# A graph-attention and four-expert kernel: the maxima over partitions moved behind the experts' low parts, and every engine's order redrawn

## The chip, the cores and the metric

The kernel runs on 1 core of a Trainium2 chip. The metric is the device time of one execution in microseconds. A core has four computing engines, each with its own instruction list that it runs strictly in the order written: TensorE (PE, matrix products), VectorE (DVE), ScalarE (ACT) and GpSimd (POOL). SyncE (SP) only issues DMAs here. The engines meet at semaphores.

## The reference

Four batches of 512 rows with 512 features go through a two-layer graph attention over a context of 512 x 128, and then through a feed-forward part in which row 4g+e belongs to expert e:

```
x = x + xattn(ctx, adj=layernorm(x), W0, ..., W1, ...)      # two attention layers, 8 heads of 64
n = layernorm(x)
gate, up = split(n[rows of e] @ gate_up[e])                 # 512 x 1024 for each of 4 experts
x = x + (silu(gate) * up) @ down[e]
```

The adjacency is the layernormed x, and the mask added to the attention's logits is 1e10 times (adj - 1). A row's softmax therefore puts all its weight on the place of the largest x in that row, wherever the gap to the second largest is big enough. The kernel uses that: it computes y = elu(elu(ctx W0 + b0) W1 + b1) for all rows, finds each row's largest entry, and gathers from y twice by index. On the side it proves that this holds for every row (a bound made of the largest absolute values of the inputs, against each row's gap). A flag with the number of rows so proved decides at the end whether a general program must run; with these inputs it does not.

## The kernel before, in words

**Numbers.** A float32 product is made of three fast products of split numbers: each operand is cut into a high part (a cast) and a low part (the rest), and high x high, high x low and low x high are added. So every operand costs one cast (on ACT: `r_high`, `h_high`, `turned_xn`, `inner_high`) and one subtraction (on DVE or POOL: `r_low`, `h_low`, `turned_low`, `inner_low`), and each 128 x 512 result of depth 512 takes twelve matmuls. "A twelve" is such a group below.

**Stages.** (1) Layer 0, `layer0(b, c)`: 16 products of 128 x 512 for h; ACT and DVE make elu of them (`h_exp_of`, `h_below`, `h_value`). (2) Layer 1, `layer1(n)`: 16 twelves; n = 4b+t is a block of 128 rows of batch b. A bank is first filled by ACT with the bias (`seed`), and ACT and DVE make y (`y_exp_of`, `y_value`), which SP stores to a table in memory (`store_y`). (3) DVE finds the largest entry of each row of x (`find_top`, `find_row`, `rows`). POOL issues the indirect DMAs: `follow(b, e)` reads the index of an index, `gather(b, e)` reads rows of the y table and adds them to x of batch b, expert e. (4) For each expert e and batch b: DVE's `x2_stats`, `x2_moments`, POOL's `x2_inverse(e, b)` (the inverse root of the variances; for e > 0 one call serves b and b+1), DVE's `normalize(e, b)`, PE's `turn_xn` (a transpose), ACT's `turned_xn` and DVE's `turned_low`. (5) The experts. Expert 0 is done batch by batch (`first_gate`, `first_up`, `first_inner`, `turn_inner`, `first_down`), so that it can begin when one batch is there; experts 1 to 3 take all four batches in a piece (`gate(e, c)`, `up(e, c)`, `inner(e, c)`, `down_of(e, i)`, `last_down(e, b)`, `output(e, b)`).

**Weights.** 24 blocks of 512 KB, `load_r(r)`, go through a ring of 9 slots. Block r takes the slot of block r-9 and is loaded only when PE has done with that one. Blocks 0 to 5 are of expert 0, 6 to 11 of expert 1, and so on; blocks 9 and 10 are the third and fourth gate-up block of expert 1, 11 is the second half of its down weights, and 12 and 13 are the first two gate-up blocks of expert 2.

**The proof's inputs.** SP loads ctx, W1, W0 and the small vectors again (`again_ctx`, `again_w`); DVE takes maxima along rows (`ctx_maximum`, `small_maxima`), and POOL's `all_maxima` takes them over the 128 partitions with two `partition_all_reduce` calls. x is loaded again too (`again_x(b)`, then `x_stats`). `check_rows` on DVE uses all of it, late in the program.

**What sets the order.** Each engine's list of calls is written out by hand-written statements, one call per line, and so are the `pe.wait_ge` lines between PE's calls and the tables of banks. Tables of numbers say which low parts DVE makes; POOL makes the rest.

Of the kernel before, what the change touches and what calls it, by code (L numbers as in the profile page):

```python
# [20 lines left out]
F32 = mybir.dt.float32  # L21
# [355 lines left out]
def build(nc, x, ctx, W0, a_self0, a_neigh0, b0, W1, a_self1, a_neigh1, b1, gate_up, down, out,  # L377
# [19 lines left out]
    with ExitStack() as stack:  # L397
# [114 lines left out]
        Z_BANK = (2, 4, 7, 2, 7, 3, 0, 4, 6, 2, 6, 1, 6, 2, 5, 0)  # L512
        Y_BANK = (5, 1, 0, 7, 1, 5, 2, 0, 4, 1, 7, 4, 2, 1, 7, 5)
        XN_BANK = (0, 6, 3, 5, 4, 5, 0, 7, 4, 5, 6, 7, 4, 5, 6, 7)
        GATE_BANK = (0, 4, 6, 6, 4, 6, 4, 6, 4, 6, 4, 6, 4, 6, 4, 6)
        UP_BANK = (6, 0, 4, 3, 5, 7, 5, 7, 5, 7, 5, 7, 5, 7, 5, 7)
        IN_BANK = (6, 3, 1, 7)
        DOWN_BANK = (2, 2, 2, 0, 0, 1, 2, 3, 0, 1, 2, 3, 0, 1, 2, 3)
# [120 lines left out]
        def _(sp):  # L639
# [60 lines left out]
            load_r(0)  # L700
            load_b1(0)
            load_w(1)
            load_r(1)
            load_ctx(1)
            load_ctx(2)
            load_r(6)
            load_w(2)
            load_r(4)
            load_x(0)
            load_r(2)  # L710
            load_r(8)
            load_ctx(3)
            load_x(3)
            load_x(1)
            load_x(2)
            load_r(3)
            load_r(5)
            store_y(0)
            store_y(1)
            store_y(2)  # L720
            load_r(7)
            store_y(3)
            store_y(4)
            store_y(5)
            store_f(0)
# [3 lines left out]
            store_f(2)  # L729
            store_y(8)  # L730
            store_y(9)
            store_y(10)
            store_y(11)
            store_y(12)
            store_y(13)
            store_y(14)
            store_f(3)
            store_y(15)
            again_ctx()
            again_w()  # L740
# [5 lines left out]
            load_r(11)  # L746
            again_x(0)
            load_r(15)
            store_out(0, 2)
            load_r(16)  # L750
            again_x(1)
            load_r(14)
            load_r(13)
            store_out(0, 3)
            load_r(18)
            again_x(2)
            load_r(19)
            load_r(17)
            again_x(3)
            load_r(21)  # L760
            load_r(22)
            store_out(1, 0)
            load_r(20)
            store_out(1, 1)
            store_out(1, 2)
            store_out(1, 3)
            load_r(23)
# [12 lines left out]
        def _(pool):  # L780
# [63 lines left out]

            r_low(0)
            r_low(1)
            h_low(1, 0)
# [5 lines left out]
            h_low(2, 1)  # L853
            h_low(2, 2)
            r_low(3)
            r_low(4)
            r_low(6)
            follow(0, 0)
            h_low(2, 3)
            follow(1, 0)  # L860
            follow(1, 1)
            gather(0, 0)
            gather(1, 0)
            h_low(3, 0)
            follow(1, 2)
            follow(2, 0)
            follow(2, 1)
            x2_inverse(0, 0)
            follow(0, 1)
            x2_inverse(0, 1)  # L870
            follow(0, 2)
            gather(2, 0)
            gather(0, 1)
            gather(1, 1)
            gather(2, 1)
            x2_inverse(0, 2)
# [3 lines left out]
            follow(0, 3)  # L880
            gather(3, 0)
            gather(3, 1)
            follow(3, 2)
            follow(3, 3)
            gather(1, 2)
            x2_inverse(0, 3)
            gather(0, 3)
            follow(1, 3)
            x2_inverse(1, 0)
            x2_inverse(1, 2)  # L890
            follow(2, 2)
            gather(1, 3)
            follow(2, 3)
            gather(2, 2)
            gather(3, 2)
            x2_inverse(2, 0)
            gather(2, 3)
            gather(3, 3)
            all_maxima()
            x2_inverse(2, 2)  # L900
            r_low(9)
            inner_low(1, 0)
            r_low(10)
            x2_inverse(3, 0)
            r_low(11)
            r_low(12)
            x2_inverse(3, 2)
            r_low(13)
            r_low(14)
# [288 lines left out]
        def _(dve):  # L1198
# [16 lines left out]
            def h_value(b, c):  # L1215
# [5 lines left out]
                else:  # L1221
                    dve.wait_ge(h_rest, n - KC + 1)
                    if n == KC:
                        dve.wait_ge(b0_made, 1)
# [734 lines left out]
```

## Time and profile before

| | us |
|---|---|
| median of 3 runs | 237.5 (235.0 to 239.65) |
| time of the profiled execution | 237.21 |
| its span, first to last instruction | 235.4 |
| PE busy | 208.7 (89%) |
| DVE / POOL / ACT busy | 152.6 / 112.6 / 98.9 |

The profiled execution is 0.3 us under the median, and its span leaves 1.8 us of its time outside. The page cuts the span into 40 slices of 5.9 us, where a digit is a busy share in tenths. PEclk is the clock granted to TensorE; 9 stands for full speed and 5 for half. The chain lists, in order of time, the work that each thing waited for, back from the end; "issue" is a time for which the profile shows no cause.

### The profile page before, as it was taken

What the parts mean: (1) busy time and instruction counts of PE and PEld (TensorE: products, weight loads), DVE (VectorE), ACT (ScalarE), POOL (GpSimd) and SP (SyncE); (2) the same over time, 40 slices, a digit from 0 to 9 for tenths busy, and PEclk for the clock granted to TensorE, in tenths of its full rate; (3) what the DMA queues carried; (4) which work ended last, traced back from release to release, by engine and by line L of the source; (5) the groups of instructions that cost most, each with busy time, mean ns of one, the idle gap of its engine ahead of it and who ended that gap; (6) DMA issues with size and microseconds to landing.
All of it is one profiled execution on the core that took longest, in us unless ns stands there. A gap on an engine that the chain in (4) does not pass through costs nothing.

```text
span 235.4 us, 2762 instructions
## 1 busy us (share of the span) xinstructions
PE 208.7 (89%) x918; PEld 163.4 (69%) x918; DVE 152.6 (65%) x283; ACT 98.9 (42%) x155; POOL 112.6 (48%) x87
## 2 busy tenths in 40 slices
PE   7989999999998979999800599999999999999990
PEld 3446777768877857888700488888888888888870
DVE  0689999998996369986203997796892633422231
ACT  2899999996533211502350012816216132222100
POOL 2324577989888679585014880621354820020000
PEclk9999999999999999999965599999999999999997
DMA  6999991216449899469940059846263021111005
GB/s 203 354 410 421 410 338 52 90 48 128 140 93 198 192 195 259 95 127 271 325 173 0 0 157 363 265 143 235 89 221 140 0 89 46 45 47 45 0 30 156
DMA packets 15202, 38.78 MB, mean 165 GB/s; under 512 B 2768, under 2 KB 2768, under 8 KB 14160
## 3 DMA queue, kind: packets, MB, share of 16 engines
q1 hardware_dynamic: 12080, 34.10, 40.8%
q0 software_dynamic: 2816, 4.20, 11.7%
q10 hardware_dynamic: 288, 0.26, 0.3%
q8 instruction: 8, 0.13, 0.2%
q14 instruction: 10, 0.08, 0.2%
HBM read 30.16 MB, written 8.40 MB: 164 GB/s over the span
## 4 chain that ended last, share of the span: by engine, by line
PE 44%; DVE 18%; issue 15%; DMA 10%; POOL 8%; ACT 3%; POOLq 0%; SPq 0%
PE bank L1690 25%; PE bank L1704 14%; POOL x_sb L819 4%; DMA y_table<-val 4%; DVE found L1254 3%; DVE top L1250 3%; DVE hexp L1225 3%; DVE val L1244 3%; DMA ff_row<-f_table,f_row 2%; DMA val<-in_ctx 2%; DMA x_sb<-y_table,ff_row 2%; POOL ff_row L807 2%; PE bank L1734 2%; PE bank L1677 1%; PE bank L1640 1%
## 5 line engine op out<-in xcount | busy, mean ns | idle before, releaser
L1690 PE MATMUL bank<-acts,ring 128*128 128x512 f32 x288 | 69.8, 399 | 14.9 <-DVE first_parts L1295 14.9
L1690 PEld LDWEIGHTS bank<-acts,ring 128*128 128x128 f32 x288 | 55.3, 193 | 26.8 <-DVE first_parts L1295 15.1
L794 POOL TENSOR_TENSOR ring<-ring_raw,ring 128x1024 fp32r<-128x1024 f32 x15 | 36.6, 2460 | 27.7 <-ACT ring L930 27.7
L1626 PE MATMUL bank<-wide,acts 128*128 128x512 f32 x192 | 48.9, 408 | 0.6 <-ACT bank L963 0.4
L1626 PEld LDWEIGHTS bank<-wide,acts 128*128 128x128 f32 x192 | 35.7, 188 | 12.3 <-issue 3.1
L1704 PE MATMUL bank<-ring,wide 128*128 128x512 f32 x144 | 34.5, 391 | 0.0
L930 ACT CAST ring<-ring_raw 128x1024 fp32r<-128x1024 f32 x24 | 24.5, 1053 | 16.2 <-DMA ring_raw<-in_down_t 9.3
L1704 PEld LDWEIGHTS bank<-ring,wide 128*128 128x128 f32 x144 | 26.9, 188 | 5.5
L819 POOL DMA_INDIRECT x_sb<-y_table,ff_row x16 | 25.8, 1613 | 8.1 <-issue 3.3
L1026 ACT CAST wide<-hexp 128x512 fp32r<-128x512 f32 x12 | 7.5, 621 | 42.0 <-DVE hexp L1304 42.0
L1651 PE MATMUL bank<-ring,first_xnT 128*128 128x512 f32 x96 | 23.0, 394 | 1.2 <-DVE first_xnT L1284 1.2
L833 POOL TENSOR_TENSOR wide<-hexp,wide 128x512 fp32r<-128x512 f32 x6 | 7.9, 1315 | 31.1 <-ACT wide L1026 31.1
L1276 DVE TENSOR_SCALAR xn<-x_sb,x2mv,rstd 128x512 f32<-128x512 f32 x16 | 11.3, 732 | 16.3 <-POOL rstd L827 15.0
L1651 PEld LDWEIGHTS bank<-ring,first_xnT 128*128 128x128 f32 x96 | 17.7, 188 | 5.0 <-DVE first_xnT L1284 1.4
L807 POOL DMA_INDIRECT ff_row<-f_table,f_row x16 | 18.7, 1171 | 4.2 <-issue 3.6
L1317 DVE SCALAR_TENSOR_TENSOR x_sb<-x_sb,bank 128x512 f32<-128x512 f32 x16 | 10.9, 687 | 12.4 <-PE bank L1704 11.8
L1614 PE MATMUL bank<-ctxT,W_f 128*128 128x512 f32 x32 | 16.8, 624 | 1.3 <-DVE hexp L1219 1.3
L1304 DVE TENSOR_TENSOR hexp<-bank,hexp 128x512 f32<-128x512 f32 x12 | 8.2, 686 | 14.5 <-PE bank L1690 14.5
L1015 ACT ACTIVATE hexp<-bank 128x512 f32<-128x512 f32 x12 | 7.1, 595 | 21.3 <-PE bank L1690 21.3
L1208 DVE TENSOR_TENSOR ring<-ring_raw,ring 128x1024 fp32r<-128x1024 f32 x9 | 13.0, 1462 | 4.4 <-ACT ring L930 4.4
L800 POOL TENSOR_TENSOR acts<-hexp,acts 128x512 fp32r<-128x512 f32 x9 | 12.1, 1370 | 6.5 <-ACT acts L954 6.5
L969 ACT ACTIVATE yexp<-bank,minus_one 128x512 f32<-128x512 f32 x16 | 10.9, 708 | 5.1 <-PE bank L1626 5.1
(87 smaller groups left out, 250.7 us busy)
## 6 DMA issues: line engine op xcount, KB each, us to landing
ring_raw<-in_gate_up_t SPq DMA_DIRECT2D x16, 512.0 KB, 6.4
ring_raw<-in_down_t SPq DMA_DIRECT2D x8, 512.0 KB, 8.0
x_sb<-in_x SPq DMA_DIRECT2D x4, 1024.0 KB, 16.4
y_table<-val SPq DMA_DIRECT2D x16, 256.0 KB, 3.5
out<-x_sb SPq DMA_DIRECT2D x16, 256.0 KB, 2.8
val<-in_x SPq DMA_DIRECT2D x4, 1024.0 KB
ctxT<-in_ctx_t SPq DMA_DIRECT2D x4, 256.0 KB, 8.0
wide_raw<-in_W_t SPq DMA_DIRECT2D x2, 512.0 KB, 8.3
```

Of the source, the lines that this page charges most:

```text
L794: nc.gpsimd.tensor_tensor(ring[:, r % RING, LO, :], ring_raw[:, r % RING, LO, :], ring[:, r % RING, HI, :].bitcast(F32), ALU.subtract).the ...
L800: nc.gpsimd.tensor_tensor(hT[:, b % 2, c, LO, :], hexp[:, n % HEXP, :], hT[:, b % 2, c, HI, :].bitcast(F32), ALU.subtract).then_inc(h_lo_p ...
L807: nc.gpsimd.indirect_dma_start(out=ff_row[:, b, e:e + 1], out_offset=None, in_=f_table[b][:, :], in_offset=bass.IndirectOffsetOnAxis(ap=f_ ...
L819: nc.gpsimd.indirect_dma_start(out=x_sb[:, b, e, :], out_offset=None, in_=y_table[b][:, :], in_offset=bass.IndirectOffsetOnAxis(ap=ff_row[ ...
L930: nc.scalar.copy(ring[:, r % RING, HI, :], ring_raw[:, r % RING, LO, :]).then_inc(r_hi, 1)
L1208: nc.vector.tensor_tensor(ring[:, r % RING, LO, :], ring_raw[:, r % RING, LO, :], ring[:, r % RING, HI, :].bitcast(F32), ALU.subtract).the ...
L1276: nc.vector.tensor_scalar(xn[:, b, :], x_sb[:, b, e, :], x2mv[:, e, b, 0:1], rstd[:, e, b:b + 1], ALU.subtract, ALU.mult).then_inc(xn_made, 1)
L1614: nc.tensor.matmul(bank[Z_BANK[n]][:, :], W0_f[:, c * P:(c + 1) * P], ctxT[:, b, :], start=True, stop=True).then_inc(h_done, 1)
L1626: last = nc.tensor.matmul(bank[Y_BANK[n]][:, :], hT[:, b % 2, c, w, t * P:(t + 1) * P], W1p[:, c, v, :], start=False, stop=(c == KC - 1 an ...
L1651: last = nc.tensor.matmul(bank[(UP_BANK if half else GATE_BANK)[b]][:, :], first_xnT[:, b % 2, k, w, :], ring[:, 0:KC, v, (half * KC + k) ...
L1690: last = nc.tensor.matmul(bank[(UP_BANK if half else GATE_BANK)[KC * e + c]][:, :], ring[:, r % RING, w, col:col + P], xnT[:, (e - 1) % 2, ...
L1704: last = nc.tensor.matmul(bank[DOWN_BANK[B * e + b]][:, :], inner_parts[:, i, w, b * P:(b + 1) * P], ring[:, r % RING, v, (i % 2) * D:(i % ...
```

## The change

Four things are edited; nothing that is computed changes.

1. **POOL's order.** `all_maxima()` stands behind `x2_inverse(2, 2)`, `x2_inverse(3, 0)`, `x2_inverse(3, 2)` and `r_low(9)`, `r_low(10)`, `r_low(12)`, and ahead of `r_low(13)`, `r_low(14)` and the rest. The four `gather(b, 3)` and the `follow` calls move forward.
2. **All other orders.** PE runs `first_gate(0)` between the parts of `layer1(12)`; expert 0's last down products and expert 1's parts are laid out anew. SP loads the ring's blocks in another order, several of them behind `store_y(0)` to `store_y(3)`. ACT runs `first_silu(0)` ahead of `y_exp_of(12)`. The banks are given out anew.
3. **Who makes low parts.** Ring blocks: DVE 9 to 11, POOL 15 to 13. Expert parts of experts 1 to 3: DVE 6 to 8, POOL 6 to 4. h: DVE 7 to 8, POOL 9 to 8.
4. **Batch 0's h.** `h_below` of h(0, 1) and h(0, 3) goes from DVE to ACT, which changes the sign in which these two are kept.

```diff
-        R_LO_DVE = (5, 7, 8, 15, 16, 17, 18, 19, 23)
-        H_LO_DVE = (0, 1, 2, 3, 13, 14, 15)
-        IN_LO_DVE = (5, 6, 10, 12, 14, 15)
+        R_LO_DVE = (1, 3, 5, 6, 7, 8, 11, 15, 19, 20, 23)
+        H_LO_DVE = (0, 1, 2, 3, 9, 10, 14, 15)
+        IN_LO_DVE = (4, 5, 6, 7, 8, 9, 10, 11)
+        BELOW_DVE = (0, 2)
...
-                if b == 0:
-                    nc.scalar.mul(hT[:, 0, c, HI, :], hexp[:, c, :], -1.0).then_inc(h_hi, 1)
+                if n in BELOW_DVE:
+                    nc.scalar.mul(hT[:, b % 2, c, HI, :], hexp[:, n % HEXP, :], -1.0).then_inc(h_hi, 1)
...
             gather(3, 3)
-            all_maxima()
-            x2_inverse(2, 2)
             r_low(9)
-            inner_low(1, 0)
             r_low(10)
+            x2_inverse(2, 2)
             x2_inverse(3, 0)
-            r_low(11)
-            r_low(12)
             x2_inverse(3, 2)
+            r_low(12)
+            all_maxima()
             r_low(13)
             r_low(14)
```

**POOL, from the last gathers to the end of its list.** `x_sb<-y_table3` is a gather of batch 3, `rstd` an `x2_inverse`, `ring` an `r_low`, `wide` an `inner_low`; the ISA rows beside `allmax` and `allsum` change POOL's configuration for the two reduces and back. Before:

```order
L819 DMA x_sb<-y_table2,ff_row 128x512
L819 DMA x_sb<-y_table3,ff_row 128x512
L842 ISA
L842 ISA allmax<-rowmax 128x4
L843 ISA allsum<-rowsum 128x5
L827 ISA
L827 TENSOR_TENSOR rstd<-veps,minus_half 128x2
L794 TENSOR_TENSOR ring<-ring_raw,ring 128x1024
L833 TENSOR_TENSOR wide<-hexp,wide 128x512
```

And of the change:

```order
L820 DMA x_sb<-y_table3,ff_row 128x512 x2
L828 TENSOR_TENSOR rstd<-veps,minus_half 128x2
L795 TENSOR_TENSOR ring<-ring_raw,ring 128x1024 x2
L828 TENSOR_TENSOR rstd<-veps,minus_half 128x2 x3
L795 TENSOR_TENSOR ring<-ring_raw,ring 128x1024
L843 ISA
L843 ISA allmax<-rowmax 128x4
L844 ISA allsum<-rowsum 128x5
L795 ISA
L795 TENSOR_TENSOR ring<-ring_raw,ring 128x1024 x7
```

All inverse roots now precede the two reduces; behind them come seven low parts of the ring, of which the first is block 13.

**DVE, from expert 1's first product to `first_inner_low(3)`.** `acts<-bank` is a `turned_low`, `ring` an `r_low` (block 11), `xn` a `normalize`, `hexp<-bank` an `inner(1, c)`, `rowsum` and `rowmax` the maxima along rows. Of the change:

```order
L1286 TENSOR_TENSOR acts<-bank5,acts 128x4x128
L1207 TENSOR_TENSOR ring<-ring_raw,ring 128x1024
L1278 TENSOR_SCALAR xn<-x_sb,x2mv,rstd 128x512
L1306 TENSOR_TENSOR hexp<-bank7,hexp 128x512
L1278 TENSOR_SCALAR xn<-x_sb,x2mv,rstd 128x512
L1330 TENSOR_REDUCE rowsum<-yexp 128x1
L1332 TENSOR_REDUCE rowsum<-val 128x4
L1335 TENSOR_REDUCE rowmax<-yexp 8x1 x2
L1337 TENSOR_REDUCE rowmax<-b0_col 128x1
L1278 TENSOR_SCALAR xn<-x_sb,x2mv,rstd 128x512 x2
L1306 TENSOR_TENSOR hexp<-bank5,hexp 128x512
```

Before, the maxima of rows came ahead of `first_inner(3)`, and the low part of block 11 was POOL's. Now `r_low(11)` stands ahead of `normalize(2, 2)` and `inner(1, 1)`, and `small_maxima` behind them.

## Rows read from the trace of the kernel before

**Rows 1.** The page: span, and busy tenths of PE and its clock in 40 slices.
```profile
span 235.4 us, 2762 instructions
...
PE   7989999999998979999800599999999999999990
...
PEclk9999999999999999999965599999999999999997
```
**Rows 2.** Waits of PE: who waited for whom, total us, times, longest.
```profile
PE bank L1690 <- DVE first_parts L1295: 14.9, 1, 14.9
...
PE bank L1666 <- DVE first_sil L1290: 1.4, 1, 1.4
...
PE bank L1651 <- DVE first_xnT L1284: 1.2, 1, 1.2
```
**Rows 3.** The chain of waits about the hole: start us, us, what.
```profile
109.91 8.62 issue
118.53 0.39 POOL allmax L842
118.91 0.45 POOL allsum L843
...
119.43 7.12 issue
126.55 0.74 POOL rstd L827
...
131.29 0.61 DVE first_parts L1295
...
131.94 5.05 PE bank L1690 x12
...
139.75 2.73 PE bank L1690 x12
```
**Rows 4.** Busy us by stretch: PE, PEld, DVE, ACT, POOL, clock, DMA share, GB/s.
```profile
110.00:120.00 10.00, 7.06 (x38) 5.71 (x36) 2.36 (x7) 5.42 (x7) 0.83 (x2) 0.96 1.05 353
120.00:130.00 10.00, 0.00 (x0) 0.00 (x0) 2.68 (x2) 1.13 (x3) 3.45 (x3) 0.50 0.02 9
```
**Rows 5.** Timeline of PE: two places ahead of the hole.
```profile
19.98 4.78 PE L1626 MATMUL bank<-wide,acts 128*128 128x512 f32 x18
...
101.94 2.88 PE L1651 MATMUL bank<-ring,first_xnT 128*128 128x512 f32 x12
```
**Rows 6.** Timeline of SP: the issue of ring blocks 9, 10, 12; of x, again.
```profile
104.85 1.38 SPq L663 DMA_DIRECT2D ring_raw<-in_gate_up_t  x3
...
159.60 0.33 SPq L697 DMA_DIRECT2D val<-in_x  x1
```
**Rows 7.** Timeline of ACT: a table load; the casts of blocks 11 and 12.
```profile
71.03 1.28 ACT L995 ACT_TABLE_LOAD   x1
...
117.68 1.99 ACT L930 CAST ring<-ring_raw 128x1024 fp32r<-128x1024 f32 x2 [3.45 <-DMA ring_raw<-in_down_t]
```
**Rows 8.** Timeline of DVE: first and last of 5 row maxima; x_stats(3, e).
```profile
103.02 0.68 DVE L1328 TENSOR_REDUCE rowsum<-yexp 128x1 f32<-128x512 f32 x1
...
106.19 0.13 DVE L1335 TENSOR_REDUCE rowmax<-b_col 128x1 f32<-128x4 f32 x1
...
165.87 2.46 DVE L1342 BATCH_NORM_STATS2 x2stat<-val 128x6 f32<-128x512 f32 x4
```
**Rows 9.** Instructions on a tile: duration ns, min/median/max; first, last start.
```profile
L1276 DVE TENSOR_SCALAR xn<-x_sb,x2mv,rstd x16: 525/542/2570, 63.4 to 143.5; 128x512 f32<-128x512 f32 x16
...
L1208 DVE TENSOR_TENSOR ring<-ring_raw,ring x9: 1209/1219/3418, 48.3 to 195.2; 128x1024 fp32r<-128x1024 f32 x9
...
L794 POOL TENSOR_TENSOR ring<-ring_raw,ring x15: 2329/2403/2849, 8.5 to 184.4; 128x1024 fp32r<-128x1024 f32 x15
```
**Rows 10.** The page's DMA issues: KB each, median us from issue to landing.
```profile
ring_raw<-in_gate_up_t SPq DMA_DIRECT2D x16, 512.0 KB, 6.4
```
**Rows 11.** The chain of waits, front part: the third batch's first gather.
```profile
66.44 5.19 DMA x_sb<-y_table,ff_row
```

More of the change, by code:

```diff
@@ L1047, in _ @@
             w_high(2)
+            h_exp_of(1, 1)
+            h_exp_of(1, 2)
+            h_exp_of(1, 3)
             h_below(1, 0)
-            h_exp_of(1, 1)
-            h_high(0, 3)
-            h_exp_of(1, 2)
             h_below(1, 1)
             h_below(1, 2)
+            h_below(1, 3)
+            y_exp_of(0)
             h_high(1, 0)
-            h_exp_of(1, 3)
+            r_high(0)
+            act.wait_ge(y_made, 1)
+            seed(2)
             h_high(1, 1)
-            h_below(1, 3)
+            y_exp_of(1)
@@ L1083, in _ @@
             seed(7)
-            seed(8)
+            h_below(2, 3)
+            h_high(2, 1)
+            y_exp_of(5)
             h_high(2, 2)
             r_high(3)
+            h_high(2, 3)
+            seed(8)
+            y_exp_of(6)
+            seed(9)
             r_high(4)
-            y_exp_of(5)
             r_high(5)
+            y_exp_of(7)
+            act.wait_ge(y_made, 7)
+            seed(10)
+            act.wait_ge(h_made, 12)
+            seed(11)
             r_high(6)
-            y_exp_of(6)
@@ L1462, in _ @@
             x2_moments(0, 1)
-            r_low(8)
-            normalize(0, 0)
-            y_value(12)
-            normalize(0, 1)
+            h_low(3, 3)
             find_top(3, 1)
@@ L1469, in _ @@
             find_row(3, 1)
+            normalize(0, 1)
             find_row(3, 2)
+            find_top(3, 3)
+            r_low(5)
+            y_value(12)
+            find_row(3, 3)
             y_value(13)
-            find_top(3, 3)
-            find_row(3, 3)
+            rows(3)
+            r_low(6)
+            x2_stats(0, 2)
             y_value(14)
-            rows(3)
-            turned_low(0, 0)
-            x2_stats(0, 2)
             x2_moments(0, 2)
+            r_low(7)
             y_value(15)
             turned_low(0, 1)
+            r_low(8)
             normalize(0, 2)
@@ L1489, in _ @@
             x2_moments(0, 3)
-            x2_moments(1, 0)
             x2_stats(1, 1)
             x2_stats(1, 2)
+            first_inner_low(1)
+            x2_stats(1, 3)
             normalize(0, 3)
-            x2_stats(1, 3)
-            first_inner(2)
+            x2_moments(1, 0)
             x2_moments(1, 1)
@@ L1498, in _ @@
             x2_moments(1, 3)
-            turned_low(0, 3)
-            first_inner_low(1)
+            output(0, 0)
             normalize(1, 0)
-            output(0, 0)
             normalize(1, 1)
+            first_inner(2)
             normalize(1, 2)
             normalize(1, 3)
-            first_inner_low(2)
+            turned_low(0, 3)
             x2_stats(2, 0)
+            output(0, 1)
             x2_stats(2, 1)
@@ L1511, in _ @@
             turned_low(1, 2)
+            turned_low(1, 3)
             x2_moments(2, 0)
-            turned_low(1, 3)
-            output(0, 1)
             x2_moments(2, 1)
-            small_maxima()
+            x2_stats(2, 2)
+            ctx_maximum()
+            x2_moments(2, 2)
             first_inner(3)
@@ L1519, in _ @@
             normalize(2, 1)
-            x2_stats(2, 2)
             x2_stats(2, 3)
-            x2_moments(2, 2)
-            x2_moments(2, 3)
             x2_stats(3, 0)
-            inner(1, 0)
-            normalize(2, 2)
-            normalize(2, 3)
-            first_inner_low(3)
             x2_stats(3, 1)
@@ L1564, in _ @@
             x_stats(2, 3)
-            r_low(17)
-            r_low(18)
-            r_low(19)
-            inner(2, 0)
+            inner(2, 1)
+            r_low(20)
+            inner_low(2, 1)
+            inner(2, 2)
+            inner_low(2, 2)
             x_stats(3, 0)
```

604 lines of the change are left out of this document (299 added, 305 removed).

## Prediction

> **What bounds the kernel now.** I began with the page. PE's slices are at 8 or 9 tenths nearly everywhere but for one hole past the middle (8, 0, 0, 5), where PEclk falls to 5 and 6 [rows 1]. So the kernel is bound by PE, less a hole, and the first question is what made it. The waits of PE name it: once, 14.9 us, for DVE's `first_inner_low(3)`; the next largest waits are 1.4 and 1.2 us [rows 2]. That name is only the last link, so I read the chain there. POOL comes to `all_maxima` at 109.9: 8.6 us of nothing, the two reduces with under 1 us between them, 7.1 us of nothing again, and only then, at 126.5, `x2_inverse(2, 2)`, 0.7 us. DVE had stood before `normalize(2, 2)` for it, with `first_inner_low(3)` behind, which ends at 131.9, and PE goes on [rows 3]. The reduces thus hold POOL from 109.9 to 126.5, 16.6 us, and all of PE's hole is behind them. Nothing needs their result there: `check_rows` is far down. The hole costs more than its width, since the clock stood at 0.50 in it [rows 4] and the first twelve matmuls after it took 5.05 us, where a twelve takes 2.73 later: 2.3 us [rows 3].
>
> **The change, part by part.**
>
> *The reduces leave the way of the inverse roots.* PE's wait goes: -14.9, and with it the slow twelve: -2.3. Together -17.2. What is late next must be looked for in two places: behind the reduces' new place, and ahead of the old one, where all orders are new.
>
> *Behind the new place.* I count from the end of `first_up(3)`, T, which is 104.7 before (101.94 and a twelve) [rows 5]. From T to `gate(2, 1)`, the first reader of block 13, the new PE order has 16 twelves (counting 4 `last_down` as one) and 10 transposes of four matmuls, which I take at 0.4 (an estimate from 128 columns against 512 and the start of each): 16 x 2.73 + 4.0 = T+47.7. POOL's side: the reduces wait for `small_maxima`. Ahead of it on DVE stands `r_low(11)`, which needs block 11. Blocks 9 to 12 were issued from 104.85, and ACT began to cast 11 and 12 at 117.7, T+13 [rows 6, 7]. So the cast ends at T+14, `r_low(11)` takes 1.2 to 3.4 [rows 9], say 2.4 beside a busy POOL: T+16.4. `normalize(2, 2)`, `inner(1, 1)`, `normalize(2, 3)` add some 1.7 by their medians: T+18.1. The row maxima take 3.3 (103.02 to 106.32) [rows 8]: T+21.4. The reduces then take 16.6: T+38.0. `r_low(13)` takes 2.4: T+40.4. Against T+47.7 that is 7.3 us of slack, so the 16.6 us are hidden by PE's own work, and cost 0. The next low parts, blocks 14, 16, 17, follow 2.4 us apart, while PE wants a new block at most every 5.4. If this cover went, each us would count.
>
> *`x2_inverse(2, 2)` is now behind blocks 9 and 10.* Two `r_low` of 2.4 [rows 9] begin when those are cast, some 6 us after their issue and a cast of 1 us later [rows 10, 7], so it ends near T+13. DVE stands before block 11 until T+14 anyway. PE's deadline for `inner(1, 1)` is `gate(1, 3)`, at T+20.4 by the same counting (7 twelves, 3 transposes); it is made at T+17.5. Slack 2.9 us: cost 0.
>
> *x again.* `x_stats(0, 0)` now stands before `output(0, 3)`, for which PE waits at `down_of(1, 0)`, T+30.5. Its load follows the row maxima, T+21.4. The nearest row is x's last reload: issued at 159.6, used without a wait at 165.9, so at most 6.3 us [rows 6, 8]: T+27.7, and 1.4 for the two DVE steps: T+29.1. Cost 0 to 5.1 (the upper end if it takes 12.8, as blocks 9 to 12 did until ACT's cast). I take 0.5, since the like transfer is the nearer row.
>
> *The front.* Between the second half of `layer1(0)` at 19.98 [rows 5] and T, PE has the same work as before, less one transpose (0.4), plus one layer-0 product that now comes later. Walking through it with the durations of before, I find six short waits, 3.4 us together: `seed(2)` 0.7, `h_low(3, 1)` 0.5, `seed(15)` 0.8, `turned_low(0, 1)` 0.3, `normalize(0, 3)` 0.7, `first_inner(2)` 0.4. Before had about 3.2 of such. The first parts of `layer1` start some 3 us earlier, but the second half of W1 is cast and split no earlier than before, and there the gain ends. So the front is 0. Its bounds: -3.2 if no wait is left, and +6 if one gather more comes into PE's way (5.2 us from issue to landing [rows 11], and a DVE step): `x2_stats(0, 0)` and `x2_stats(0, 2)` now stand before `y_value(8)` and `y_value(14)`, on which ACT's seeds and so PE hang.
>
> *ACT's tables.* `first_silu(0)` ahead of `y_exp_of(12)` makes two more table loads of 1.28 us each [rows 7]. Only the first lies ahead of something near its time, `y_value(13)` and `seed(15)`, where DVE is as late. 0.4 us at most, and inside the 0.8 above. The Trainium skill's "ScalarE: Activation LUTs", section "What ACT_TABLE_LOAD costs", has 2.66 us for each switch, a drain included; no row here shows the drain. By it `seed(15)` would come another 1.4 us later, and the sum would be 1.4 more.
>
> *Low parts, batch 0's h, the end.* Four more low parts on DVE, five fewer on POOL, two more `h_below` on ACT: all beside PE. In experts 2 and 3 every deadline that I followed has over 5 us, since PE is full there [rows 1], and `last_down(3, 3)` and `output(3, 3)` end the program as before. 0.
>
> **Sum.** Against the profiled execution's own time, 237.2 (span 235.4 and 1.8 around; 0.3 under the median): 237.2 - 14.9 - 2.3 + 0.5 + 0 = **220.5 us**, 7% below the median.
>
> **Rivals.** Under 232.8 is faster by 2% and over 242.2 slower by 2%, which is about what this kernel's runs, 235.0 to 239.65, can tell.
>
> *A. The reduces bind in their new place.* Their 16.6 us lie mostly in the two voids. If moved between loads these doubled, `r_low(13)` would be 15.7 - 7.3 = 8.4 us late: 228.9. For: the DMA share is 1.05 and 353 GB/s in the new place's kind of traffic. Against: the first void lay in just that traffic, the second in near silence (9 GB/s), and they are 8.6 and 7.1 [rows 3, 4]. Chance 0.08.
>
> *B. DVE and POOL get in each other's way.* One `normalize` took 2.57 us with a median of 0.54, one `r_low` on DVE 3.42 with 1.22 [rows 9]. In the stretch T+8 to T+18 POOL makes blocks 9, 10 and 12 and DVE block 11 and two `normalize`. If each of the three is held for a POOL operation of 2.4, that is 7.2, of which one 1.2 is counted and 2.9 is slack: +3.1, and 223.6; once more around `inner_low(1, c)`, 226. The Trainium skill's "SBUF — State Buffer", section "Who interferes with whom", says that a DVE instruction with two SBUF inputs and a GpSimd one that reads SBUF shut each other out for a whole instruction. The rows agree in kind. Chance 0.10.
>
> *C. The front slips by a gather*, as bounded above: +6, 226.5. For: two gathers stand in DVE's line before work that PE needs. Against: my walk has both landing within 1 us of need. Chance 0.10.
>
> *D. The change does not do what it says*: the hole only moves. It would need A and C together, or blocks 9 to 12 some 12 us later than before ahead of `x2_inverse(2, 2)`. Then -17.2 is nearly given back: 233 to 237. Against: PE frees their slots at the same T. Chance 0.05.
>
> *E. Slower: the reduces hold seven low parts.* All of POOL's blocks of experts 2 and 3 are behind them. They decide from 16.6 + 7.3 = 23.9 us on, and to pass 242.2 must cost another 21.7, so take over 45.6 us, nearly three times the row. If they did, 243. Chance 0.02.
>
> The forecast keeps 0.65. **Range:** 215.5 (220.5 less 3.2, less the small waits that remain, some 1.8) to 229 (A's end, with B and C inside): D and E and some tails are left out, under 0.2. **Chances:** faster 0.92 (forecast, A, B, C), same 0.05, slower 0.03 (E, and what I have not thought of).
>
> **What would show it.** PE's waits hold no entry over 6 us, PEclk stays at 9 between the front and the end. The voids about `allmax` are still some 8 and 7 us, with PE busy throughout. `gate(2, 1)` starts without a wait, over 5 us after `r_low(13)` ends. `first_up(3)` ends at 104 to 105. PE's last matmul is at 212 to 213. I am wrong if PE waits for a `ring` low part behind the reduces (A, E), for `inner` or `output` near T+20 to T+30 (B, or x's reload), or if T is beyond 108 (C).

## The result, and the profile after

The changed kernel takes **221.39 us** (median of 4 runs, 220.26 to 221.66) where the kernel before takes 237.09 beside it (235.0 to 239.65): ratio 0.9356, 95% interval 0.9281 to 0.9432. The forecast was 220.5, range 215.5 to 229. The profiled run is the one of 221.66 us, with a span of 219.8 against 235.4; its granted clock is 0.998 of full speed. All medians here are over every run of a version, while a ratio leaves out runs that lie over 1.5% above the fastest of their version.

The page after, to be set against [rows 1]. The hole in PE is gone, and PEclk stays at 9:

```profile
span 219.8 us, 2740 instructions
...
PE 206.4 (94%) x907; PEld 160.9 (73%) x907; DVE 154.1 (70%) x286; ACT 103.3 (47%) x159; POOL 102.4 (47%) x82
...
PE   7998899979979899999999999999999999999990
...
PEclk9999999999999999999999999999999999999999
```

The waits of PE after, against [rows 2]: who waited for whom, total us, times, longest. These six rows are all:

```profile
PE bank L1631 <- POOL acts L801: 1.8, 3, 1.2
PE bank L1631 <- ACT bank L959: 1.6, 2, 1.0
PE bank L1739 <- POOL ones L784: 1.5, 1, 1.5
PE bank L1631 <- DVE wide L1201: 1.0, 1, 1.0
PE bank L1656 <- DVE first_xnT L1286: 1.0, 1, 1.0
PE bank L1645 <- DVE xn L1278: 0.8, 1, 0.8
```

The third is the start of the program. The other eight waits, 6.2 us together, all lie in the front, before 83 us. From 82.94 to the last matmul, which ends at 214.1, the chain of waits runs through PE alone. Below is PE's timeline (start, busy us, line, what, count). The first line ends with `first_up(3)`, so T = 105.8; the second begins with `gate(2, 1)`, the first reader of block 13; the third is the end:

```profile
100.14 5.70 PE L1656 MATMUL bank<-ring,first_xnT 128*128 128x512 f32 x24
...
153.77 13.76 PE L1695 MATMUL bank<-acts,ring 128*128 128x512 f32 x60
...
213.14 0.96 PE L1709 MATMUL bank<-ring,wide 128*128 128x512 f32 x3
```

`gate(2, 1)` starts at T+48.0 (forecast T+47.7), and no wait stands in front of it. The reduces are still on POOL, between two stretches of low parts. This is POOL's timeline, with the idle time before a row, and what ended it, in brackets:

```profile
112.64 4.75 POOL L795 TENSOR_TENSOR ring<-ring_raw,ring 128x1024 fp32r<-128x1024 f32 x2 [8.24 <-ACT ring L926]
117.35 2.98 POOL L828 TENSOR_TENSOR rstd<-veps,minus_half 128x2 f32<-128x2 f32 x3
120.31 2.62 POOL L795 TENSOR_TENSOR ring<-ring_raw,ring 128x1024 fp32r<-128x1024 f32 x1
128.65 0.39 POOL L843 PARTITION_ALL_REDUCE allmax<-rowmax  x1 [5.72 <-issue]
128.96 0.53 POOL L844 PARTITION_ALL_REDUCE allsum<-rowsum  x1
140.33 7.49 POOL L795 TENSOR_TENSOR ring<-ring_raw,ring 128x1024 fp32r<-128x1024 f32 x3 [10.85 <-ACT ring L926]
```

The reduces have a void (an idle stretch) of 5.7 us ahead and one of 10.9 behind. The second is not theirs alone: what ended it is ACT's cast of block 13, at 140.2. With the 7.1 us that the void behind the reduces took before [rows 3], POOL would have been free at about 136.6, 3.7 us ahead of the block. So after the change the load of block 13 is what `r_low(13)` waits for, and the reduces lie inside that wait. `r_low(13)`, some 2.5 of the 7.49, ends at 142.8, 11 us before `gate(2, 1)`.

### The profile page after: what moved, and what is told of

It is laid out like the page before. It is cut to its first block, busy times and chain, and to the rows that moved or that the text cites. A ratio compares the mean times of both kernels' runs of the same rounds, so it can differ in the third digit from the quotient of the medians.

```text
span 219.8 us, 2740 instructions
## 1 busy us (share of the span) xinstructions
PE 206.4 (94%) x907; PEld 160.9 (73%) x907; DVE 154.1 (70%) x286; ACT 103.3 (47%) x159; POOL 102.4 (47%) x82
## 4 chain that ended last, share of the span: by engine, by line
PE 62%; DVE 17%; POOL 6%; ACT 5%; DMA 4%; issue 4%; POOLq 0%; DVEq 0%
PE bank L1695 30%; PE bank L1709 15%; PE bank L1656 6%; PE bank L1682 5%; DVE found L1256 4%; DVE hexp L1227 4%; DVE val L1246 3%; DVE top L1252 3%; PE bank L1645 3%; DMA f_table<-f_row 3%; ACT hexp L933 2%; POOL ff_row L808 2%; PE bank L1739 2%; POOL x_sb L820 2%; DVE f_row L1260 1%
## 5 line engine op out<-in xcount | busy, mean ns | idle before, releaser
L1695 PE MATMUL bank<-acts,ring 128*128 128x512 f32 x288 | 67.2, 390 | 0.0
L1695 PEld LDWEIGHTS bank<-acts,ring 128*128 128x128 f32 x288 | 53.9, 188 | 11.2
L795 POOL TENSOR_TENSOR ring<-ring_raw,ring 128x1024 fp32r<-128x1024 f32 x13 | 32.9, 2548 | 32.4 <-ACT ring L926 32.4
L820 POOL DMA_INDIRECT x_sb<-y_table,ff_row x16 | 25.3, 1582 | 5.3 <-issue 4.2
L808 POOL DMA_INDIRECT ff_row<-f_table,f_row x16 | 16.4, 1027 | 10.8 <-DMA y_table<-val 3.7
L801 POOL TENSOR_TENSOR acts<-hexp,acts 128x512 fp32r<-128x512 f32 x8 | 11.3, 1503 | 19.7 <-ACT acts L950 19.7
L1011 ACT ACTIVATE hexp<-bank 128x512 f32<-128x512 f32 x12 | 7.2, 598 | 23.9 <-PE bank L1695 23.8
L834 POOL TENSOR_TENSOR wide<-hexp,wide 128x512 fp32r<-128x512 f32 x4 | 5.2, 1289 | 26.5 <-ACT wide L1022 26.5
L1278 DVE TENSOR_SCALAR xn<-x_sb,x2mv,rstd 128x512 f32<-128x512 f32 x16 | 12.7, 821 | 5.1 <-POOL rstd L828 5.1
L1619 PE MATMUL bank<-ctxT,W_f 128*128 128x512 f32 x32 | 16.2, 632 | 0.0
L1207 DVE TENSOR_TENSOR ring<-ring_raw,ring 128x1024 fp32r<-128x1024 f32 x11 | 15.7, 1431 | 0.0
L965 ACT ACTIVATE yexp<-bank,minus_one 128x512 f32<-128x512 f32 x16 | 10.9, 690 | 3.3 <-PE bank L1631 3.2
```

The lines of the kernel that those rows point to most:

```text
L795: nc.gpsimd.tensor_tensor(ring[:, r % RING, LO, :], ring_raw[:, r % RING, LO, :], ring[:, r % RING, HI, :].bitcast(F32), ALU.subtract).the ...
L801: nc.gpsimd.tensor_tensor(hT[:, b % 2, c, LO, :], hexp[:, n % HEXP, :], hT[:, b % 2, c, HI, :].bitcast(F32), ALU.subtract).then_inc(h_lo_p ...
L808: nc.gpsimd.indirect_dma_start(out=ff_row[:, b, e:e + 1], out_offset=None, in_=f_table[b][:, :], in_offset=bass.IndirectOffsetOnAxis(ap=f_ ...
L820: nc.gpsimd.indirect_dma_start(out=x_sb[:, b, e, :], out_offset=None, in_=y_table[b][:, :], in_offset=bass.IndirectOffsetOnAxis(ap=ff_row[ ...
L1207: nc.vector.tensor_tensor(ring[:, r % RING, LO, :], ring_raw[:, r % RING, LO, :], ring[:, r % RING, HI, :].bitcast(F32), ALU.subtract).the ...
L1278: nc.vector.tensor_scalar(xn[:, b, :], x_sb[:, b, e, :], x2mv[:, e, b, 0:1], rstd[:, e, b:b + 1], ALU.subtract, ALU.mult).then_inc(xn_made, 1)
```

## Experiments

Each run is compared with runs of the kernel before on the same chip; the ratios can be set against the 0.9356 above, and those of section 5 against a second timing of the changed kernel as it is, which stands there. PE, DVE, ACT, POOL and SP are meant as in the page.

### 1. The reduces' place alone

The kernel before with one line moved on POOL:

```diff
             gather(3, 3)
-            all_maxima()
             x2_inverse(2, 2)
...
             x2_inverse(3, 2)
+            all_maxima()
             r_low(13)
```

> The kernel before with one statement moved: all_maxima() stands behind x2_inverse(3, 2) and ahead of r_low(13); every other order stays. Theory R (the reduces held the inverse roots, and nothing else of the change matters much): PE's wait of 14.9 us and the slow twelve of 2.3 us go, so 219.5 to 221, and PE's waits hold nothing over 2 us. Rival F (the other orders carry part of the gain, since in the old ones block 13 or 14 is late behind the reduces): 223 to 230, with a wait of PE for a low part of the ring at gate(2, 1) or down_of(2, 0).

Measured: 223.16 us (221.59 to 223.73), ratio 0.943 (0.9365 to 0.9495). Taken on 237.1 us, the ratios make one moved line worth 13.5 us and the whole change 15.3; the times do not separate the 1.8 between them, since the two intervals overlap. The trace says where they can lie. This is the timeline of PE in this run, with two waits past T that the changed kernel does not have:

```profile
119.17 3.02 PE L1690 MATMUL bank<-acts,ring 128*128 128x512 f32 x12 [1.75 <-DVE first_parts L1295]
...
151.33 5.70 PE L1690 MATMUL bank<-acts,ring 128*128 128x512 f32 x24 [1.01 <-POOL ring L794]
```

The first is the wait for `first_inner_low(3)` again, of which more below. The second is `gate(2, 1)` waiting for block 13 behind the reduces, in the old order of everything else: there the reduces came later (`all_maxima` to 140.8), and POOL's first low part started at 148.4. The profile names ACT's cast for that idle time of 7.6 us, but the cast of block 13 was over at 135.7, so it was the void. Past T the rest of the change, the redrawn orders, removes these two waits, 2.8 us.

### 2. Both kernels without the reduces

In each, the two reduces are replaced by two small POOL instructions that write the same tiles, so that the kernel leaves out the maxima over partitions:

```diff
-                nc.gpsimd.partition_all_reduce(allmax[:, :], rowmax[:, :], P, RMAX).then_inc(all_made, 1)
-                nc.gpsimd.partition_all_reduce(allsum[:, :], rowsum[:, :], P, RSUM).then_inc(all_made, 1)
+                nc.gpsimd.tensor_scalar(allmax[:, :], rowmax[:, :], 1.0, None, ALU.mult).then_inc(all_made, 1)
+                nc.gpsimd.tensor_scalar(allsum[:, :], rowsum[:, :], 128.0, None, ALU.mult).then_inc(all_made, 1)
```

Of the kernel before:

> The kernel before, in which the two reduces over partitions are left out: two small POOL operations on the same 4 and 5 columns stand in their place, so the proof's bound is made from one partition's maxima. Theory R: the voids of 8.6 and 7.1 us go with them, PE's hole goes, 219 to 221. Rival G (under the hole lies another late thing, ring blocks 9 to 12 or the last gathers): over 223, with PE waiting for that.

Of the changed kernel:

> The changed kernel with the two reduces left out in the same way. Theory R (they are wholly hidden in their new place): 221.4 within 0.5. Rival A (they still cost something, through block 13 or POOL's later work): 216 to 220.

Measured: before without reduces 221.39 us (219.73 to 222.03), ratio 0.9368 (0.9298 to 0.9437); after without reduces 221.02 (220.76 to 221.56), ratio 0.9357 (0.9305 to 0.9409). In the old place the reduces cost 15.0 us (13.4 to 16.6, from the ratio on 237.1); in the new one nothing that can be measured. And once they are free, the old orders and the new ones take the same time, within intervals of 1.2 to 1.7 us to either side. So PE's hole was theirs, and the gain is, as far as these intervals can tell, that they are hidden.

### 3. How much the new place can hide

The changed kernel with two more pairs right behind the first, each with a small ordinary POOL instruction ahead:

```diff
+            def again(k):
+                nc.gpsimd.tensor_scalar(between[:, k, :], rowmax[:, :], 1.0, None, ALU.mult)
+                nc.gpsimd.partition_all_reduce(allmax2[:, k, :], rowmax[:, :], P, RMAX)
+                nc.gpsimd.partition_all_reduce(allsum2[:, k, :], rowsum[:, :], P, RSUM)
...
             all_maxima()
+            again(0)
+            again(1)
             r_low(13)
```

> The changed kernel with two more pairs of reduces into unused tiles right behind the first, with a small ordinary POOL operation between pairs. Theory R (each change of configuration and back costs about what it did, 16.6 us a pair): in the changed kernel POOL is at the first reduce at 128.7 and would be ready for block 13 by 137; two more pairs bring that to 170, and the low part to 172.5, where gate(2, 1) now starts at 153.9: PE waits 18 to 19 us, and the clock falls, so 238 to 243. If the voids are not paid per change of configuration but once, or were waits for something else: 221.4 to 224.

Measured: 239.54 us (238.82 to 239.93), ratio 1.0135 (1.0077 to 1.0193). This is rival E's mechanism at work: the same kernel goes from 0.936 to 1.4% above the kernel before, by voids on one engine. This is the timeline of POOL in this run:

```profile
128.01 0.38 POOL L846 PARTITION_ALL_REDUCE allmax<-rowmax  x1 [6.12 <-issue]
128.32 0.53 POOL L847 PARTITION_ALL_REDUCE allsum<-rowsum  x1
136.06 0.26 POOL L850 TENSOR_SCALAR between<-rowmax 128x4 f32<-128x4 f32 x1 [7.21 <-issue]
143.70 0.39 POOL L851 PARTITION_ALL_REDUCE allmax<-rowmax  x1 [7.39 <-issue]
144.01 0.53 POOL L852 PARTITION_ALL_REDUCE allsum<-rowsum  x1
151.62 0.26 POOL L850 TENSOR_SCALAR between<-rowmax 128x4 f32<-128x4 f32 x1 [7.08 <-issue]
158.82 0.39 POOL L851 PARTITION_ALL_REDUCE allmax<-rowmax  x1 [6.95 <-issue]
159.13 0.53 POOL L852 PARTITION_ALL_REDUCE allsum<-rowsum  x1
167.15 6.99 POOL L798 TENSOR_TENSOR ring<-ring_raw,ring 128x1024 fp32r<-128x1024 f32 x3 [7.49 <-issue]
```

And this is its chain of waits, from the end of `small_maxima` to the first void, and at PE's first matmuls behind the wait (start us, us, what):

```profile
123.71 4.31 issue
...
169.62 16.25 PE bank L1705 x60
```

Each added pair costs POOL 15.1 to 15.7 us, of which the reduces are under 1. The rest is a void of 7.0 to 7.4 us at each change from ordinary instructions to a reduce, and one of 7.1 to 7.5 back. The tiny `between` (0.26 us) is enough to pay both. POOL is free for `r_low(13)` at 167.15; without the two pairs it would be at about 136.1, where the first `between` starts. That is 31 us, of which PE waits 16.8: the new place hid 14.3 us of them, the 3.7 to the load of block 13 and the 11 of slack behind `r_low(13)`, within 1 us. From the end of `small_maxima` to `r_low(13)` POOL is held for 43.4 us here (123.71 to 167.15), so PE begins to wait at 26.6; the prediction had 23.9. The granted clock was 0.64 in the wait (153.0 to 169.6) and 0.84 in the sixty matmuls behind it, which took 16.25 where the same sixty take 13.60 in the chain of the changed kernel: 2.65 us, the second appearance of the prediction's term of 2.3.

### 4. The wait without the fall of the clock

The kernel before, with 130 small matmuls into a free bank (`keep_on`, which the kernel has at other places too) ahead of PE's wait, to part the prediction's two terms, -14.9 and -2.3:

```diff
             turn_xn(2, 1)
+            keep_on(130, 3)
             pe.wait_ge(first_in_lo, 4)
```

> The kernel before, with 130 small matmuls into a bank that is free put in front of TensorE's wait for the transposed low parts behind the reduces (up(1, 1)), so that the engine is busy through the wait of 14.9 us and its clock should not fall. The prediction's sum has two separate terms for this hole: 14.9 us of waiting and 2.3 us for the twelve slow matmuls behind it. By that only the 2.3 us go: 234 to 235.5 us, the chain of waits still led through the reduces, and the next stretch of twelve at full pace (about 3.0 us where it took about 5.3). The rival: the slow matmuls cost nothing by themselves, since what follows them is held by later work anyway (casts, loads); then the time stays at 237 and a wait of about 2 us appears further on.

Measured: 234.31 us (233.38 to 236.63), ratio 0.9894 (0.9847 to 0.994): 2.5 us less, between 1.4 and 3.6. The hole is filled, and the granted clock is 1.00 from 119.1 to 133.4, the 2.4 GHz level, where it stood at 0.50, the 1.2 GHz level, in the hole before [rows 4]. The timeline of PE:

```profile
119.06 14.36 PE L1728 MATMUL bank<-ident,ones_bf 128*128 128x256 bf16 x130
133.59 3.06 PE L1690 MATMUL bank<-acts,ring 128*128 128x512 f32 x12 [0.18 <-DVE first_parts L1295]
136.49 2.88 PE L1677 MATMUL bank<-ring,first_parts 128*128 128x512 f32 x12
```

The twelve behind the hole take 3.06 where they took 5.05 [rows 3]. The wait is as long as ever, now with other work in it, and only the second payment, for the clock, is gone. The two terms of the sum are separate, and both real.

### 5. The front

After the result was known, the front of the changed kernel looked like the part furthest off the forecast: eight waits of 6.2 us where the walk had six of 3.4. In the trace of the changed kernel one DVE instruction stands out, `rows(2)` on 128x4 numbers. Timeline of DVE, and of POOL at that time:

```profile
57.66 3.09 DVE L1260 TENSOR_SCALAR f_row<-found 128x4 uint32<-128x4 uint32 x1
```

```profile
57.63 3.08 POOL L801 TENSOR_TENSOR acts<-hexp,acts 128x512 fp32r<-128x512 f32 x2
```

The other three `rows` took 0.16 to 0.9 us. This one started 0.03 us after POOL's two low parts and ended with them: it was held for their whole length. That is rival B's mechanism in a place where the prediction had not looked. The rule of the Trainium skill ("SBUF — State Buffer", section "Who interferes with whom") is that, when the two engines want the shared ports, the one to issue first has them for its whole instruction. The 3.09 beside 3.08 agree in kind; here VectorE was held over two POOL instructions in a row.

Two edits, one at a time: `rows(2)` three steps later on DVE, and `first_silu(0)` behind `turned_xn(0, 1)` on ACT, which also takes away two table loads.

```diff
             h_value(3, 2)
-            rows(2)
             find_row(3, 0)
             h_value(3, 3)
             turned_low(0, 0)
+            rows(2)
             h_low(3, 2)
```

> The changed kernel with rows(2) on DVE moved from before find_row(3, 0) to behind turned_low(0, 0). In the changed kernel it took 3.09 us where rows() takes 0.45 to 0.9, and began 0.03 us after POOL's two h_low. Theory P (DVE was shut out by a POOL operation that had begun; what stands behind it on DVE, h_value(3, 3) and turned_low(0, 0), came 2.5 us late and PE waited 1.0 and 0.4 us for it): PE's wait for first_xnT goes, 0.5 to 1.5 us less than the control. Rival (the time only moves, since the index DMAs of batch 2 start later and PE waits for them): equal to the control within 0.4.

```diff
             seed(14)
-            first_silu(0)
             y_exp_of(12)
...
             turned_xn(0, 1)
+            first_silu(0)
             first_silu(1)
```

> The changed kernel with first_silu(0) on ACT moved behind y_exp_of(15), as before: two table loads of 1.28 us fewer. Theory of the prediction (DVE is as late as ACT there): equal to the control within 0.4 us. Rival (ACT's tables set seed(15), for which PE waited 0.64): 0.4 to 0.7 less, and the wait of PE for ACT's bank goes.

Measured: `rows(2)` later 220.06 us (219.1 to 221.44), ratio 0.9323 (0.9275 to 0.937), the moved `rows` now 1.19 us; `first_silu(0)` later 220.93 (220.26 to 221.45), ratio 0.9353 (0.9311 to 0.9396). The changed kernel itself, timed again beside them:

> The changed kernel as it is, on the same chip as the three above: 221.4 within 0.5, by every theory.

It took 220.44 us (219.71 to 222.51), ratio 0.9331 (0.9283 to 0.9379). So neither edit can be told from no edit. In the trace of the first, the wait of 1.0 at the first gate is 0.6 and the one for `xn` 0.3 where it was 0.8. But in the trace of the kernel timed again, where `rows(2)` took 3.11, they are 0.5 and 0.7, so these differences are not shown to come from the edit. Nor was `rows(2)` set free by it. Timeline of DVE, and of POOL, with `rows(2)` later:

```profile
58.38 1.19 DVE L1260 TENSOR_SCALAR f_row<-found 128x4 uint32<-128x4 uint32 x1
```

```profile
56.43 3.10 POOL L801 TENSOR_TENSOR acts<-hexp,acts 128x512 fp32r<-128x512 f32 x2
```

It ends with POOL's pair again (59.57 and 59.53), and is shorter only because it starts later. The instructions that now stand ahead of it beside the same pair, one `find_row`, `h_value(3, 3)` and `turned_low(0, 0)`, took 0.68, 0.73 and 0.68 us, as elsewhere.

For the second edit it is what the prediction had: the two extra table loads cost the kernel nothing measurable, and PE's waits for ACT's banks are 1.6 us with them and without. In the changed kernel the load ends and the next exponential starts with nothing between (timeline of ACT):

```profile
66.20 1.28 ACT L991 ACT_TABLE_LOAD   x1
...
68.12 1.28 ACT L965 ACT_TABLE_LOAD   x1
69.41 1.27 ACT L965 ACTIVATE yexp<-bank,minus_one 128x512 f32<-128x512 f32 x2
```

The Trainium skill's price of 2.66 us for each switch ("ScalarE: Activation LUTs", "What ACT_TABLE_LOAD costs"), by which the prediction's sum would have been 1.4 more, is not what these rows show: 1.28, and no drain after it.

Then six such moves at once: those two, `seed(2)` ahead of `r_high(0)`, `y_value(12)` and `(13)` ahead of `r_low(5)`, `h_low(2, 3)` ahead of `follow(0, 2)`, and, on POOL, this one:

```diff
             gather(0, 2)
+            x2_inverse(0, 2)
             follow(3, 0)
             follow(3, 1)
-            x2_inverse(0, 2)
             follow(3, 2)
```

> The changed kernel with both moves and four more, each at a place where PE waited in the front: r_high(0) behind seed(2) on ACT; r_low(5) and find_row(3, 3) behind y_value(13) on DVE; h_low(2, 3) ahead of follow(0, 2) and x2_inverse(0, 2) ahead of follow(3, 0) on POOL. If the six front waits (6.2 us) are each of their own, some 4 us go: 217 to 218.5, and first_up(3) ends at 101 to 102. Rival (the waits stand in for one another: the chain of y stores and gathers to batch 3 sets when normalize(0, 3) can run, and PE only waits there instead): 220 to 221, with a wait of PE of 2 to 4 us for xn of batch 3.

Measured: 221.91 us, over 218.07 to 225.17, too scattered for a ratio. The lowest run is in the first theory's range, and the one with a trace, 222.4, shows the rival's wait, at a longer time than it had. There PE was 2.5 to 4.4 us ahead of the changed kernel until 90, and then lost it in one wait of 3.3 for batch 3's first `normalize`, with the granted clock at 0.66 behind it (94 to 99). Timeline of POOL in this run:

```profile
83.25 0.95 POOL L808 DMA_INDIRECT ff_row<-f_table,f_row  x1 [3.70 <-DMA ff_row<-f_table,f_row]
84.50 1.60 POOL L820 DMA_INDIRECT x_sb<-y_table,ff_row  x1 [0.30 <-issue]
...
92.39 1.16 POOL L828 TENSOR_TENSOR rstd<-veps,minus_half 128x1 f32<-128x1 f32 x1
```

`follow(3, 2)` waits there for the landing of an index read and stands ahead of `gather(3, 0)`, on which PE hangs; `x2_inverse(0, 3)` comes behind two more gathers. That gives an edit that can be tested, in this run's kernel and in the one with `rows(2)` alone:

```diff
             follow(3, 1)
-            follow(3, 2)
             gather(3, 0)
             gather(3, 1)
+            follow(3, 2)
             follow(3, 3)
+            x2_inverse(0, 3)
             gather(1, 2)
             gather(2, 2)
-            x2_inverse(0, 3)
             gather(0, 3)
...
             x2_stats(0, 3)
+            x2_moments(0, 3)
             x2_stats(1, 0)
-            x2_moments(0, 3)
```

With all six moves:

> The changed kernel with all the moves of the run that shifted six steps of the front (rows(2), first_silu(0), r_high(0), r_low(5), h_low(2, 3), x2_inverse(0, 2)), and with four more for batch 3's chain, which bound there: on POOL gather(3, 0) and gather(3, 1) ahead of follow(3, 2), x2_inverse(0, 3) ahead of gather(1, 2) and gather(2, 2), on VectorE x2_moments(0, 3) right behind x2_stats(0, 3). If POOL's order made that chain late, gather(3, 0) starts about 1.6 us earlier and x2_inverse(0, 3) about 3 us earlier, the 3.3 us wait at turn_xn(0, 3) falls under 1 us, the first expert's up products of batch 3 end by 103, and the time is 217 to 219. The rival: the index's read and the gather itself (their landing) set it, whatever the order; then the wait stays over 2 us and the time at 220 to 222.

With `rows(2)` and `x2_inverse(0, 2)` alone:

> The changed kernel with rows(2) behind turned_low(0, 0) and the moves for batch 3's chain (x2_inverse(0, 2) ahead of follow(3, 0), gathers (3, 0) and (3, 1) ahead of follow(3, 2), x2_inverse(0, 3) ahead of gathers (1, 2) and (2, 2), x2_moments(0, 3) earlier), without the other five moves of the front. There TensorE comes to turn_xn(0, 3) later than in the run above, and that chain is in time already: by that theory the moves save only the wait at normalize(0, 2), and the time is as with rows(2) alone, 219.5 to 220.5. The rival: batch 3's chain costs time in the changed kernel too; then 218 or less.

Measured: all together 221.8 us median of 7 runs, 218.91 to 224.27, three of them at 218.9 to 219.1. Its ratio, 0.926 (0.9211 to 0.9309), rests on the four lowest, so the spread is the better guide here. The smaller set took 219.79 (219.38 to 220.14), ratio 0.9291 (0.9257 to 0.9325), as its theory had it; the rival's 218 or less did not come.

The larger edit did what it was meant to in the run that has a trace, the one of 221.8: `gather(3, 0)` starts at 81.34, not 84.50, `x2_inverse(0, 3)` at 89.28, not 92.39, and the wait at `turn_xn(0, 3)` is gone. The median is in the rival's range, but not by the rival's wait: another took its place. PE and DVE of that run:

```profile
78.63 4.58 PE L1656 MATMUL bank<-ring,first_xnT 128*128 128x512 f32 x12 [3.08 <-DVE first_xnT L1286]
```

```profile
74.59 0.69 DVE L1265 BATCH_NORM_STATS2 x2stat<-x_sb 128x6 f32<-128x512 f32 x1 [2.79 <-DMA x_sb<-y_table,ff_row]
75.20 0.67 DVE L1246 SCALAR_TENSOR_TENSOR val<-yexp,bank 128x512 f32<-128x512 f32 x1
...
77.80 0.68 DVE L1286 TENSOR_TENSOR first_xnT<-bank,first_xnT 128x512 fp32r<-128x512 f32 x1
```

And its chain of waits has the transfer that did it:

```profile
67.06 7.28 DMA x_sb<-y_table,ff_row
```

This gather took 7.28 us from issue to landing, against 5.19 in [rows 11], and `x2_stats(0, 2)` stood before it with `y_value(14)` and `turned_low(0, 1)` behind. That is rival C as the prediction worded it, in a kernel that is a little earlier than the changed one. In the changed kernel the same gather was issued at 68.64, and `x2_stats(0, 2)` follows at 73.59 without a wait. So in the two hurried fronts that have a trace PE lost its lead to a small transfer, once an index read and once a gather. Whether the front's length is set in this way in every run was not tried. The smaller set is the best version that ran steadily: its runs lie within 0.8 us, and its median is the lowest of all. Its interval overlaps that of the changed kernel, so that it is better is not shown.

## Why the prediction was right

The traces allow a finer cut than the times. T and the rest of the span, in us:

| trace | T | from T to the end |
|---|---|---|
| before | 104.8 | 130.6 |
| one line moved (1) | 105.2 | 116.7 |
| before, without reduces (2) | 104.0 | 115.2 |
| before, matmuls in the hole (4) | 107.0 | 127.8 |
| changed | 105.8 | 114.0 |
| changed, without reduces (2) | 105.8 | 113.9 |
| changed, three pairs (3) | 104.8 | 133.3 |
| changed, timed again (5) | 106.7 | 114.0 |

The five edited fronts of section 5 have T from 103.0 to 106.5, and 113.9 to 114.2 behind it. So in the changed kernel the part behind T hardly differs from one execution to the next, and nearly all of the difference between executions lies ahead of T. Behind T, by one trace for each version, the moved line alone is worth 13.9 us and the redrawn orders another 2.7; the reduces cost 15.4 in the old place and 0.1 in the new one.

**The wait goes, -14.9.** Right, by the waits of PE (none over 1.2 us past the start) and by section 2: 15.0 us for the reduces in their old place, slow matmuls and all. The two terms together were 17.2. Most of the 2.2 between is a wait that the reduces had covered: without them PE still waits 1.6 us for `first_parts` in the old order, in the kernel of section 2. The timeline of DVE there shows why, `normalize(2, 2)` and `normalize(2, 3)` ahead of `first_inner_low(3)`:

```profile
113.48 3.77 DVE L1276 TENSOR_SCALAR xn<-x_sb,x2mv,rstd 128x512 f32<-128x512 f32 x2
117.17 0.68 DVE L1295 TENSOR_TENSOR first_parts<-bank,first_parts 128x512 fp32r<-128x512 f32 x1
```

Two of them take 1.1 us by their median; beside POOL's `r_low(9)` and `inner_low(1, 0)` they took 3.77, and with 1.1 PE would not have waited. It is the same in section 1 (3.75). In the new orders they took 0.55 and 0.54.

**The slow twelve, -2.3.** Right: 2.5 us (1.4 to 3.6) by section 4, and 2.8 by the part behind T.

**The new place, 0.** Right, and with more slack than the walk had. `small_maxima` ended at T+18.4, not T+21.4 (`r_low(11)` started at T+11.2 and took 1.4, where the walk had T+14 and 2.4). The void ahead of the reduces began at 122.9, before `small_maxima` ended at 124.3, so only 4.4 us of it lay behind that end, where the walk had put all of its 8.6. POOL was free of the reduces near T+31, not T+38. The load of block 13, which the walk had not followed, then took the lead, and the slack was 11 us for 7.3. That this load was in time too is luck, since the prediction had not looked at it. Section 2 prices the reduces there at nothing. By section 3 PE begins to wait once POOL is held for 26.6 us from the end of `small_maxima` on (43.4 less 16.8), where rival E had 23.9.

**`x2_inverse(2, 2)` behind blocks 9 and 10, 0.** Right: POOL's three `rstd` run from T+11.5, the walk had the first ending near T+13, and PE does not wait there.

**x again, +0.5.** It was 0. Issued at 124.31, used at 133.12 by a DVE that had its other work until then, and `output(0, 3)` behind it waited 1.13 us for PE, not PE for it.

**The front, 0.** The term held within what can be told, and the walk behind it did not. T is 105.8 here, not 104 to 105, and 1.0 later than before. But with the same front it was 105.8, 104.8 and 106.7 in three more traces, and with the front of before 104.0 to 107.0 in four, so this 1.0 is not shown to be the change's. In the pair of traces, PE's work up to T shrank by 0.7 us (98.77 to 98.10 busy) and its waits grew by 1.7: from 4.5 (`hexp` 1.3, `first_sil` 1.4, `first_xnT` 1.2 and two under 0.5) to 6.2, both without the first of the program. Of the walk's six waits the seeds (1.6 for 1.5) and `h_low(3, ...)` (0.6 for 0.5) are there. `turned_low` and `normalize` are too, but each one batch earlier than the walk had them, 1.0 for 0.3 and 0.8 for 0.7; `first_inner(2)` is not. Missed were the split of W1 (1.0) and `h_low(2, 3)` (1.2). One thing out of the ordinary was found there, the held `rows(2)`, and no run shows that it costs the kernel anything.

**The end.** From T on the kernel takes 114.0 us of span where it took 130.6. That is 16.6 less, and the forecast had 16.7. With the front's +1.0 the sum of the profiled executions is -15.6. PE's last matmul ends at 214.1, where the prediction had 212 to 213: that is the late T.

**The rivals.** A and E were told apart from the forecast by the same number, the length of the voids in the new place. They did not double between the loads (5.7, and at most 10.9 with a load in it; in section 1 10.4), and in section 3 they are 6.1 ahead of the first reduce and 7.0 to 7.5 after that. How near A was shows in section 1: with a first void of 10.4 and the old orders around it, PE lost 1.0 us there. D is refuted by PEclk and by the waits. B and C exist, where the prediction had not priced them or where they cost PE nothing. B held `rows(2)` in the front, and the two `normalize` in the old order. In the stretch where it was priced, nothing was held (`r_low(11)` 1.40, `normalize` 0.55 and 0.54), but just behind it, beside `r_low(13)` and its followers, two `normalize` took 5.25 us together and an `r_low` 3.42, and PE did not wait. C was met only in a hurried front of section 5.

One term of the range has no source: the last 1.8 us of its lower end, for small waits that remain, come from no row.

## What to carry to other kernels

When an engine's custom instruction leaves a void, price the void and not the instruction: here 0.9 us of work held POOL for 16.6 us. Then look for a place with that much slack to the next reader of whatever the engine makes, and count in the time that the next piece of its work is late anyway, because that part of the void is free. And one moved line gave 13.5 of 15.3 us by the times, 13.9 of 16.6 behind T: before redrawing all orders, try that one. Where the runs of a kernel scatter, find the stretch in which they do; here it lies ahead of T, and behind T one trace told apart a few tenths of a microsecond, which the times could not.

## What the runs showed of the hardware

- A change between ordinary POOL instructions and a partition reduce costs 7.0 to 7.5 us each way (section 3), even for an instruction of 0.26 us between them; two reduces in a row have no void between them. The void ahead of a kernel's first reduce was 5.7, 6.1, 8.7 and 10.4 us in the changed kernel, section 3, the kernel before and section 1. No run tells why it differs. The Trainium skill ("GPSIMD Engine Reference", "2.1 Instruction dispatch") has about 6 us, without an instruction in the profile, for the first call of newly loaded code; the rows of section 3 agree in kind, are 1.0 to 1.5 us longer, and show the price at every change and again on the way back.
- The two reduces took 0.39 and 0.53 us in the changed kernel, and 1.42 and 1.28 in section 1. No run tells why.
- A DVE instruction on 128x4 numbers took 3.09 us when it started 0.03 us behind two POOL low parts, and 1.19 when it started 1.95 us behind them: both times it ended with them. Instructions of DVE that read a bank, or only search x, kept their 0.7 us beside the same pair.
- The same gather took 5.19 us from issue to landing in the kernel before and 7.28 in section 5; the store of four columns of row numbers took 6.22 us (`f_table<-f_row`, batch 3, in the changed kernel). The runs of one version differ by 0.8 to 7 us, and by the traces most of that lies ahead of T. That such transfers make it was not tried.
